# The tail of three attention layers: value blocks, first batch's ending, holding matmuls and a fourth score bank reordered

## The chip, the cores and the metric

The kernel runs on one core of a Trainium2 chip. The metric is the time of one execution on the device in microseconds (us); below that stand times of instructions in one profiled execution, counted from the start of its span. TensorE (PE) does matmuls and transposes into the eight banks of PSUM, VectorE (DVE) and ScalarE (ACT) read these banks, GpSimd (POOL) works in SBUF only, and SyncE (SP) issues most of the DMAs.

## What is computed

The reference is a stack of four blocks on tokens x (2 batches, 512 tokens, 256 wide) with a context of 2 x 1024 rows. Each block adds a gated cross attention and a gated feed-forward part, both on a layer norm of x:

```
x = x + tanh(g_xattn[l]) * attention_l(layernorm(x), context)
x = x + tanh(g_ffn[l])   * ffn_l(layernorm(x))
```

Attention 0 is a windowed one and is not touched. Attentions 1, 2 and 3 are ordinary softmax attentions of 512 queries over 1024 keys, with 16, 16 and 8 heads of 8, 16 and 4 channels, then an output product. The parts behind them are a top-1 mixture of 8 experts (after 1), a gated unit with three hidden layers (after 2) and a token-shift mix (after 3).

## The kernel before

**Tiling.** An attention layer goes through its heads in groups of two (16, 16 and 8 groups; groups of batch 0 first). A group has eight key tiles, called slots here, numbered through the layer: 128, 128 and 64 slots. A slot (group, tile) has two scores, one for each head, 128 keys x 512 queries. The two heads of a group lie on the two row halves of TensorE's array (64 rows each).

**The steps.** `schedule(l)` writes out one list of steps, and every engine walks through the same list and takes its own steps in that order:
- `max`: two matmuls 128 queries x 512 keys into a pair of banks 3 to 6 (L1607), reduced on VectorE (L2394). Their maxima are needed by the scores of later slots, so these products run `LEAD` = 30 scores ahead. When the last is done, the layer has 15 slots left: the tail.
- `score`: one matmul (L1631) into a bank of a ring, and one exponential on ScalarE (L1244) from it into one of six probability buffers. `ring_place()` takes the bank that has been used longest ago. There are three, 0 to 2; in the tail bank 3 joins. A score waits until the exponential that read its bank is done; the first one in bank 3 waits until all reductions of the layer are.
- `values`: a block of 16 matmuls (L1645) for two slots, summed in bank 7 over a group. It waits for the exponentials of its slots, and the first of a group for the copy of the previous group's sums.
- `copy`: ScalarE moves the sums of a group out of bank 7 (L1256), behind the eighth exponential of the next group (slot 3).
- `turned` and `normal`: after every second group the sums are transposed on TensorE (L1661) and copied by ScalarE (L1237), then GpSimd divides by the softmax sums (L976, L977).
- The ending of batch 0: `heads` (transposes of the context, L1678, one for each 128 channels: 1, 2, 1 in layers 1, 2, 3), two `out` (output product, L1705, then VectorE adds to x and takes statistics), `variance` (VectorE, then GpSimd's deviation, L910 and L911), `normalise` (VectorE, L1997) and, in layer 3, two `mix tokens` (transposes, L1686, and on VectorE copies, L2452, and the shift, L2361). These stand in the tail, where banks 4 to 6 are free: `turn()` gives out these three banks in rotation.
- `hold`: a bf16 matmul (L1614) of an identity, whose result nobody reads, in the same rotation.
- In layer 3 `mix` and `mix rest` are a gate product (L1693) that needs the shifted tokens of batch 0.

**The order.** The loop goes by two slots at a time, in the pattern `TILE_PAIR`: maxima, score, maxima, score, score, values, score. The block inside a pair is the one four slots back (`VALUES_LAG`). In the tail there is another one after the pair, when it lags three behind the second slot (`TAIL_LAG`). After the loop the rest of the blocks, the last copy, the last transpose (`context`), its normalisation on VectorE and the ending of batch 1 follow.

In layer 2 VectorE leaves the list after `normalise` of batch 0, enters the branch of the gated unit, casts the first two chunks of its weights (L2640) and takes the rest of the list after that.

Of the kernel before, what the change touches and what calls it, by code (L numbers as in the profile page):

```python
# [15 lines left out]
DC = D // P  # L16
# [23 lines left out]
HG = 2  # L40
KT = M // P
# [10 lines left out]
NGROUPS = {l: B * ATT[l][0] // HG for l in ATT}  # L52
GROUP0 = {l: sum(NGROUPS[i] for i in range(1, l)) for l in range(1, 5)}
EW = {l: ATT[l][0] * ATT[l][1] for l in ATT}
EC = {l: max(1, EW[l] // P) for l in ATT}
PREP0 = {l: sum(EC[i] * CT // CH for i in range(1, l)) for l in range(1, 5)}
QCH0 = {l: sum(EC[i] * T // CH for i in range(1, l)) for l in range(1, 5)}
RING0 = {l: sum(HG * KT * NGROUPS[i] + NGROUPS[i] // 2 - 1 for i in range(1, l)) for l in range(1, 5)}
# [28 lines left out]
CTX_BANKS0 = {0: 0, 1: 2 * DC, 2: 2 * DC + 2 * EC[1], 3: 2 * DC + 2 * EC[1] + 2 * EC[2]}  # L87
HALVES = HG * QT * 2
LEAD = HALVES + 14
VALUES_LAG, TAIL_LAG = 4, 3  # L90
TILE_PAIR = ('maxima', 'score', 'maxima', 'score', 'score', 'values', 'score')
TAIL_HOLDS = 2
WARM_FROM, LEAD_HOLDS = 2, 4
# [9 lines left out]
NORMAL_LAG = 4  # L103
# [12 lines left out]
CTX_SLOT = 7  # L116
# [21 lines left out]
def schedule(l):  # L138

    steps, turns, u, total = [], 0, 0, NGROUPS[l] * HALVES
    batch = NGROUPS[l] // B
    finish = {}
    for b in range(B - 1):
        first = NGROUPS[l] * KT - LEAD // HG + 1
        assert first > (b + 1) * batch * KT + CTX_SLOT
        for i, step in enumerate([("heads", (b, c)) for c in range(EC[l])] + [("out", (b, i)) for i in range(2)]):
            finish[first + i] = step  # L150
        last = first + EC[l] + 2
        finish[last] = ("variance", b)
        finish[last + NORMAL_LAG] = ("normalise", b)
        if l == 3:
            for c in range(DC):
                finish[last + NORMAL_LAG + 2 + c] = ("mix tokens", (b, c))

    def turn(kind, *what):
        nonlocal turns
        steps.append((kind, *what, turns))  # L160
        turns += 1

    def maxima(upto):
        nonlocal u
        while u < min(upto, total):
            steps.append(("max", u))
            u += HG
            steps.extend(LATE[l][v] for v in (u - 1, u) if v in LATE[l])
            if u % HALVES == 0:
                steps.append(("shift", u // HALVES - 1))  # L170
            if WARM_FROM <= u <= LEAD:
                steps.append(("warm",))

    valued, ring, scored = 0, 0, {}
    last_in = {k: None for k in SCORE_BANKS}

    def ring_place():

        nonlocal ring
        if u == total:  # L180
            last_in.setdefault(TAIL_SCORE_BANK, None)
        k = min(last_in, key=lambda k: (-1 if last_in[k] is None else last_in[k], SCORE_BANKS.index(k) if k in SCORE_BANKS else 0))
        before, last_in[k] = last_in[k], ring
        ring += 1
        return k, before

    def values():
        nonlocal valued
        steps.append(("values", valued // KT, valued % KT // 2, scored[valued + 1]))
        valued += 2  # L190

    def score(g, kt, hh):
        steps.append(("score", g, kt, hh, ring_place()))
        if hh < HG - 1:
            return
        sl = g * KT + kt
        scored[sl] = ring
        if kt == COPY_SLOT and g:
            steps.append(("copy", g - 1))
        if kt == CTX_SLOT and g and g % 2 == 0:  # L200
            steps.append(("turned", g - 1, ring_place()))
            steps.append(("normal", g - 1, ring))
        if sl in finish and finish[sl][0] in ("heads", "out", "mix tokens"):
            turn(*finish[sl])
        elif sl in finish:
            steps.append(finish[sl])

    for first in range(0, NGROUPS[l] * KT, 2):
        g, kt = divmod(first, KT)
        places = iter((kt + i, hh) for i in range(2) for hh in range(HG))  # L210
        pairs = iter((first, first + 1))
        for what in TILE_PAIR:
            if what == "maxima":
                maxima(LEAD + HG * next(pairs))
            elif what == "values":
                if valued + VALUES_LAG <= first:
                    values()
            else:
                t, hh = next(places)
                sl = g * KT + t  # L220
                if hh == 0 and u == total and LEAD + HG * (sl - 1) >= total and sl not in finish:
                    for _ in range(TAIL_HOLDS):
                        turn("hold")
                score(g, t, hh)
        if u == total and valued + TAIL_LAG <= first + 1:
            values()
    def first_gate(c):
        turn("mix", c)

    def second_gate(c):  # L230
        steps.append(("mix rest", *next(step[1:] for step in steps if step[:2] == ("mix", c))))

    if l == 3:
        first_gate(0)
    while valued < NGROUPS[l] * KT:
        values()
    if l == 3:
        second_gate(0)
    steps.append(("copy", NGROUPS[l] - 1))
    turn("context", NGROUPS[l] - 1)  # L240
    steps.append(("normal", *steps[-1][1:]))
    if l == 3:
        first_gate(1)
    else:
        steps.append(("tokens", 0))
    for c in range(EC[l]):
        turn("heads", (B - 1, c))
    if l == 3:
        second_gate(1)
    for i in range(2):  # L250
        turn("out", (B - 1, i))
    assert ring == RING0[l + 1] - RING0[l]
    return steps
# [56 lines left out]
def build(nc, io):  # L310
    with ExitStack() as ctx:
# [706 lines left out]
        def _(act):  # L1018
# [185 lines left out]
            def attention(l):  # L1204
# [12 lines left out]
                else:  # L1217
                    act.activation(exp_ready_table[:], onesf[0:1, 0:1], ACT.Exp)

                for step in schedule(l):  # L1220
                    if step[0] == "late tokens":
                        ln_evac(2 * l, [1], -1)
# [149 lines left out]
        def _(pe):  # L1372
# [184 lines left out]
            def attention(l):  # L1557
# [10 lines left out]
                elif l == 1:  # L1568
                    hold_clock(QUERY_HOLDS[l], 1)
                    pe.wait_ge(x_ready, stage * NT)  # L1570
                order = schedule(l)
                rotation = [step for step in order if step[0] in ("context", "heads", "out", "hold", "mix tokens", "mix")]

# [1193 lines left out]
```

## Time and profile before

| | us |
|---|---|
| median of 3 runs | 1056.04 |
| lowest, highest | 1053.68, 1060.72 |
| the profiled execution | 1049.83 |
| its span | 1047.8 |
| busy in the span: TensorE | 958.4 |
| VectorE | 748.3 |
| ScalarE | 510.0 |
| GpSimd | 286.8 |

The mean granted clock of TensorE was 0.969 of full speed (2.4 GHz). A row of instructions in order of time reads: start, time, engine, line, operation, output <- input, shape, count; then in brackets how long the engine stood idle before it, and who released it. "PEld" is the weight load that goes with a matmul. Ends of matmuls are modelled, so starts are the better measure. "Chain of waits" is the chain of work that ended last, followed back from the last instruction.

### The profile page before, as it was taken

How to read it: one execution, taken by the hardware profiler on the slowest of the kernel's cores; microseconds unless marked ns; L12 is line 12 of the kernel's file. 1: busy time of each engine (PE TensorE's matmuls, PEld its weight loads, DVE VectorE, ACT ScalarE, POOL GpSimd, SP SyncE). 2: the span in 40 equal slices, each digit the busy share in tenths (PEclk: the TensorE clock that was granted, in tenths of full speed). 3: DMA queues.
4: the chain of work that ended last, by engine and by line, in shares of the span. 5: the costliest groups of instructions: out<-in, count | busy, mean ns of one | idle time of the engine just before them, and what ended most of it. 6: DMA issues, size and time to landing. Idle time of an engine off the chain costs nothing.

```text
span 1047.8 us, 17509 instructions
## 1 busy us (share of the span) xinstructions
PE 958.4 (91%) x6560; PEld 555.9 (53%) x6560; DVE 748.3 (71%) x1125; ACT 510.0 (49%) x1028; POOL 286.8 (27%) x439
## 2 busy tenths in 40 slices
PE   9897987899999878999689999988999999889898
PEld 4333343444444355999244444444788788544346
DVE  4899888999989332454588899973664645799746
ACT  2672331588888520121027888866312212358763
POOL 3656700233343203002311443421500400023310
PEclk9999989999999977999899999999999999999999
DMA  6789912104320603995341232201254242110001
GB/s 206 248 300 312 357 32 69 43 25 128 120 89 13 182 2 116 319 381 186 101 144 47 71 93 86 52 2 42 89 192 142 83 141 102 29 46 18 2 2 40
DMA packets 79183, 121.83 MB, mean 116 GB/s; under 512 B 9733, under 2 KB 52904, under 8 KB 79090
## 3 DMA queue, kind: packets, MB, share of 16 engines
q1 hardware_dynamic: 59278, 79.29, 24.1%
q10 hardware_dynamic: 19044, 39.22, 10.7%
q0 software_dynamic: 768, 2.10, 0.6%
q8 instruction: 56, 0.92, 0.4%
q14 instruction: 37, 0.30, 0.1%
HBM read 92.10 MB, written 27.81 MB: 114 GB/s over the span
## 4 chain that ended last, share of the span: by engine, by line
PE 64%; DVE 23%; issue 4%; ACT 4%; DMA 2%; POOL 2%; ACTq 1%; DVEq 0%; SPq 0%; POOLq 0%
PE value_bank L1645 12%; PE max_bank L1874 11%; DVE arena L2394 11%; PE st_bank L1631 10%; PE max_bank L1607 7%; PE max_bank L1816 4%; PE st_bank L1804 3%; PE st_bank L1874 2%; ACT arena L1244 2%; PE max_bank L1397 1%; PE st_bank L1553 1%; PE max_bank L1705 1%; DVE arena L2106 1%; PE max_bank L1475 1%; PE st_bank L1661 1%
## 5 line engine op out<-in xcount | busy, mean ns | idle before, releaser
L2394 DVE TENSOR_REDUCE arena<-max_bank 128x2 f32<-128x1024 f32 x320 | 373.3, 1215 | 34.3 <-PE max_bank L1607 31.8
L1244 ACT ACTIVATE arena<-st_bank 128x512 f32<-128x512 f32 x616 | 327.9, 604 | 107.4 <-PE st_bank L1631 99.1
L1645 PE MATMUL value_bank<-arena,vaug 128*9 128x256 f32 (+2 forms) x2560 | 171.2, 386 | 7.8 <-ACT xnT L1256 6.0
L1631 PE MATMUL st_bank<-g_a 64*128 64x512 f32 x456 | 157.7, 447 | 0.0
L1607 PE MATMUL max_bank<-g_a 64*128 64x512 f32 x480 | 133.8, 475 | 14.1 <-DVE arena L2394 12.3
L1874 PE MATMUL max_bank<-g_a,g_w 128*128 128x512 f32 x512 | 117.3, 390 | 1.1 <-POOL g_a L995 1.1
L1631 PEld LDWEIGHTS st_bank<-g_a 64*128 64x128 f32 x456 | 75.4, 185 | 65.0 <-ACT arena L1244 59.5
L1874 PEld LDWEIGHTS max_bank<-g_a,g_w 128*128 128x128 f32 x512 | 95.9, 188 | 21.9 <-POOL g_a L995 2.0
L1645 PEld LDWEIGHTS value_bank<-arena,vaug 128*9 128x9 f32 (+2 forms) x2560 | 56.6, 92 | 85.4 <-issue 27.3
L962 POOL COPY arena<-arena 8x32 f32<-8x32 f32 x160 | 32.1, 200 | 216.6 <-DVE arena L2406 114.2
L1607 PEld LDWEIGHTS max_bank<-g_a 64*128 64x128 f32 x480 | 56.0, 185 | 57.9 <-DVE arena L2394 53.7
L976 POOL TENSOR_TENSOR arena<-arena,minus_one 128x16 f32<-128x16 f32 x17 | 49.3, 2903 | 75.5 <-ACT arena L1237 75.5
L1338 ACT ACTIVATE arena<-max_bank,arena 128x512 f32<-128x512 f32 x32 | 22.0, 688 | 91.7 <-PE max_bank L1874 91.7
L910 POOL TENSOR_SCALAR rstd<-mv 128x4 f32<-128x4 f32 x16 | 3.8, 239 | 202.9 <-DVE mv L1982 202.9
L1631 PE MATMUL st_bank<-g_a,g_x 64*128 64x512 f32 x160 | 58.8, 449 | 0.1
L2617 DVE CAST g_a<-arena 128x512 fp32r<-128x512 f32 x32 | 13.7, 427 | 58.4 <-ACT arena L1338 58.4
L1607 PE MATMUL max_bank<-g_x,g_a 64*128 64x512 f32 x160 | 42.6, 477 | 7.4 <-DVE arena L2394 2.7
L1299 ACT ACTIVATE arena<-st_bank 128x352 f32<-128x352 f32 x24 | 11.1, 464 | 75.6 <-PE st_bank L1804 75.6
L995 POOL TENSOR_TENSOR g_a<-arena,g_a 128x512 fp32r<-128x512 f32 x16 | 23.9, 1493 | 77.6 <-DVE g_a L2678 77.6
L1631 PEld LDWEIGHTS st_bank<-g_a,g_x 64*128 64x128 f32 x160 | 26.7, 189 | 26.1 <-ACT arena L1244 25.9
L1816 PE MATMUL max_bank<-arena 128*128 128x176 f32 x256 | 40.2, 315 | 0.4 <-ACT arena L1299 0.2
L1816 PEld LDWEIGHTS max_bank<-arena 128*128 128x128 f32 x256 | 38.2, 190 | 0.8 <-ACT arena L1299 0.8
(390 smaller groups left out, 1475.0 us busy)
## 6 DMA issues: line engine op xcount, KB each, us to landing
arena<-in_glu_w SPq DMA_DIRECT2D x39, 512.0 KB, 3.2
arena<-kv_table SPq DMA_DIRECT2D x11, 1024.0 KB, 8.1
ctxT<-in_glu_w ACTq DMA_DIRECT2D x22, 512.0 KB, 6.5
arena<-in_w SPq DMA_DIRECT2D x20, 512.0 KB, 6.2
kparts<-arena ACTq DMA_DIRECT2D x12, 512.0 KB, 5.5
arena<-in_w ACTq DMA_DIRECT2D x12, 512.0 KB, 3.4
xnT<-kv_table SPq DMA_DIRECT2D x5, 1024.0 KB, 7.8
g_a<-kparts SPq DMA_DIRECT2D x24, 192.0 KB
```

Of the source, the lines that this page charges most:

```text
L962: ch.link(pool.tensor_copy(mxq[0:HG * QT, r * SQ:(r + 1) * SQ], mxt[gi % 2][r * SQ:r * SQ + HG * QT, :]))
L976: ch.link(pool.tensor_tensor(rsum_p, sums[:, :, :, dh], bc(minus_one[:, 0:1].unsqueeze(2), [P, QT, 2 * HG]), ALU.pow))
L995: pool.tensor_tensor(g_a[0][1][:, f, :], g_tmp[f % 2], g_a[0][0][:, f, :].bitcast(F32), ALU.subtract).then_inc(act_split, 1)
L1244: act.activation(prob[sl % PROBS][:, hh, :], bank[k], ACT.Exp, scale=scale).then_inc(exp_ready, 1)
L1338: ins = act.activation(g_tmp[a % 2], bank[4 + f % 2], ACT.Gelu, scale=gsc[:, 1 + layer, f:f + 1])
L1607: ins = pe.matmul(max_pair[(p + FIRST_PAIR[l]) % len(max_pair)][:, hh, :], Qc[gi % KQ_BUFS][rows, qt * P:(qt + 1) * P], Kc[gi % KQ_BUFS][r ...
L1631: pe.matmul(ring_bank(*place), Kc[gi % KQ_BUFS][rows, kt * P:(kt + 1) * P], Qc[gi % KQ_BUFS][rows, :], start=True, stop=True).then_inc(st_ ...
L1645: ins = pe.matmul(bank[7][at:at + dh + 1, 0:D], vaug[l][:, b * KT + 2 * m + i, h0 + hh, :], tiles[:, a], start=(m == 0 and i == 0), stop=( ...
L1804: ins = pe.matmul(bank[i % 4][:, f % UP_PER_BANK * CAP:(f % UP_PER_BANK + 1) * CAP], mw1[wbuf][:, c, f * P:(f + 1) * P], unit_inT[n % 2][: ...
L1816: ins = pe.matmul(bank[4 + n % 2][:, c * CAP:(c + 1) * CAP], mw2[wbuf][:, f, c * P:(c + 1) * P], hid[n % 2][:, f, :], start=(f == 0), stop ...
L1874: ins = pe.matmul(out, stationary, moving, start=(first and i == 0), stop=(last and i == len(pairs) - 1))
L2394: dve.tensor_reduce(mxh[gi % 2][:, qt:qt + QT + 1:QT, half], max_pair[(p + FIRST_PAIR[l]) % len(max_pair)], AX.X, ALU.max).then_inc(max_re ...
```

## The change

All of it is in `schedule(l)`; no instruction changes but for its place in the list, its bank, and the 48 holds.

- Bank 3 joins the ring only when `tail_ring` places have been given out: not with the second score of the tail's first slot but with the eighth (second score of slot 3 of the last group but one).
- The value block after a pair of slots is gone. Only the one inside the pair stays.
- The two holds before each slot are gone.
- The ending of batch 0 was spread, one step after each slot: heads after slot 2 (and 3 in layer 2), outputs after the next two, variance after the next, normalisation four slots on, mix tokens two and three slots later. Now it stands behind pairs of slots: all heads after slot 3, both outputs after slot 5, variance after slot 7 (behind `turned` and `normal`), normalisation after slot 3 of the last group, both mix tokens after its slot 5.

```diff
-VALUES_LAG, TAIL_LAG = 4, 3
+VALUES_LAG = 4
...
-        first = NGROUPS[l] * KT - LEAD // HG + 1
-        assert first > (b + 1) * batch * KT + CTX_SLOT
-        for i, step in enumerate([("heads", (b, c)) for c in range(EC[l])] + [("out", (b, i)) for i in range(2)]):
-            finish[first + i] = step
-        last = first + EC[l] + 2
-        finish[last] = ("variance", b)
-        finish[last + NORMAL_LAG] = ("normalise", b)
+        first = NGROUPS[l] * KT // 2 - LEAD // HG // 2
+        assert 2 * first > (b + 1) * batch * KT + CTX_SLOT
+        finish[first] = [("heads", (b, c)) for c in range(EC[l])]
+        finish[first + 1] = [("out", (b, i)) for i in range(2)]
+        finish[first + 2] = [("variance", b)]
+        finish[first + 4] = [("normalise", b)]
         if l == 3:
-            for c in range(DC):
-                finish[last + NORMAL_LAG + 2 + c] = ("mix tokens", (b, c))
+            finish[first + 5] = [("mix tokens", (b, c)) for c in range(DC)]
...
+    tail_ring = RING0[l + 1] - RING0[l] - HG * (LEAD // HG - 2)
...
-        if u == total:
+        if u == total and ring >= tail_ring:
             last_in.setdefault(TAIL_SCORE_BANK, None)
...
-        if sl in finish and finish[sl][0] in ("heads", "out", "mix tokens"):
-            turn(*finish[sl])
-        elif sl in finish:
-            steps.append(finish[sl])
...
                 t, hh = next(places)
-                sl = g * KT + t
-                if hh == 0 and u == total and LEAD + HG * (sl - 1) >= total and sl not in finish:
-                    for _ in range(TAIL_HOLDS):
-                        turn("hold")
                 score(g, t, hh)
-        if u == total and valued + TAIL_LAG <= first + 1:
-            values()
+        for step in finish.get(first // 2, []):
+            turn(*step) if step[0] in ("heads", "out", "mix tokens") else steps.append(step)
```

The tail of layer 1 before and after, pair by pair (s: a score, V: a value block, numbered in the tail, h: two holds). Layer 2 has a second heads step; in layer 3 (groups 6 and 7) the mix tokens and the gate product come in addition.

```
slots      before                                            after
14.0-1     s s(bank 3) s V1 s V2                             s s s V1 s
14.2-3     s s heads s s copy out V3                         s s s V2 s(bank 3) copy heads
14.4-5     s s out s s variance V4                           s s s V3 s out out
14.6-7     h s s h s s turned normal V5                      s s s V4 s turned normal variance
15.0-1     h s s s s normalise V6                            s s s V5 s
15.2-3     h s s h s s copy V7                               s s s V6 s copy normalise
15.4-5     h s s h s s V8                                    s s s V7 s
15.6-7     h s s h s s V9                                    s s s V8 s
after      V10                                               V9 V10
```

## Rows read from the trace of the kernel before

**Rows 1.** Page: busy time of the engines, and the chain's shares by engine.
```profile
PE 958.4 (91%) x6560; PEld 555.9 (53%) x6560; DVE 748.3 (71%) x1125; ACT 510.0 (49%) x1028; POOL 286.8 (27%) x439
PE 64%; DVE 23%; issue 4%; ACT 4%; DMA 2%; POOL 2%; ACTq 1%; DVEq 0%; SPq 0%; POOLq 0%
```

**Rows 2.** Chain of waits, layer 1, before the tail: start, time, work (us).
```profile
337.43 0.98 PE value_bank L1645 x16
340.03 0.98 PE value_bank L1645 x16
```

**Rows 3.** Instructions in order of time, start of each tail: start, time; idle before.
```profile
341.71 2.36 DVE L2394 TENSOR_REDUCE arena<-max_bank 128x2 f32<-128x1024 f32 x2 [0.24 <-PE max_bank L1607]
344.12 0.49 PE L1631 MATMUL max_bank<-g_a 64*128 64x512 f32 x1 [2.10 <-DVE arena L2394]
694.87 2.36 DVE L2394 TENSOR_REDUCE arena<-max_bank 128x2 f32<-128x1024 f32 x2 [0.24 <-PE max_bank L1607]
697.28 0.50 PE L1631 MATMUL max_bank<-g_a 64*128 64x512 f32 x1 [2.10 <-DVE arena L2394]
988.49 2.36 DVE L2394 TENSOR_REDUCE arena<-max_bank 128x2 f32<-128x1024 f32 x2 [0.23 <-PE max_bank L1607]
990.90 0.50 PE L1631 MATMUL max_bank<-g_a 64*128 64x512 f32 x1 [2.08 <-DVE arena L2394]
```

**Rows 4.** Stretches, busy time by engine and clock (layers 1, 3); one block.
```profile
344.00:348.00 4.00, 3.88 (x31) 1.39 (x35) 0.45 (x3) 1.68 (x3) 1.53 (x6) 0.59 0.02 5
992.00:996.00 4.00, 3.65 (x35) 1.63 (x28) 1.20 (x2) 2.80 (x7) 1.01 (x4) 1.00 0.01 2
344.54 1.76 PE L1645 MATMUL value_bank<-arena,vaug 128*9 128x256 f32 x16
```

**Rows 5.** Order of time, layers 3 and 2: the small costs of a tail.
```profile
992.31 0.50 PE L1631 MATMUL st_bank<-g_a 64*128 64x512 f32 x1
992.74 1.05 PE L1645 MATMUL value_bank<-arena,vaug 128*5 128x256 f32 x16
998.21 1.13 PE L1705 MATMUL max_bank<-wo,xnT 32*128 32x256 f32 x4
1002.13 0.63 PE L1661 MATMUL st_bank<-ident,xnT 128*128 128x128 f32 x4 [0.16 <-ACT arena L1244]
1004.88 1.57 ACT L1244 ACTIVATE arena<-st_bank 128x512 f32<-128x512 f32 x3
704.67 1.99 PE L1705 MATMUL max_bank<-wo,xnT 128*128 128x256 f32 x8
```

**Rows 6.** Order of time, layer 1: copy, first value block of the last group.
```profile
363.05 0.47 ACT L1256 ACTIVATE xnT<-value_bank 128x256 f32<-128x256 f32 x1
363.66 1.05 PE L1645 MATMUL value_bank<-arena,vaug 128*9 128x256 f32 x16 [1.83 <-ACT xnT L1256]
```

**Rows 7.** All instructions of line L1614: shortest, median, longest in ns.
```profile
L1614 PE MATMUL max_bank<-identb x48: 376/387/388, 355.5 to 1013.1; 64*128 64x512 bf16 x48
```

**Rows 8.** Order of time: last value block of layers 1, 2 and 3.
```profile
369.69 1.05 PE L1645 MATMUL value_bank<-arena,vaug 128*9 128x256 f32 x16 [0.72 <-ACT arena L1244]
724.15 1.06 PE L1645 MATMUL value_bank<-arena,vaug 128*17 128x256 f32 x16 [0.73 <-ACT arena L1244]
1015.62 1.05 PE L1645 MATMUL value_bank<-arena,vaug 128*5 128x256 f32 x16
```

**Rows 9.** Order of time: GpSimd and VectorE in the tails of layers 3, 2.
```profile
1003.73 2.90 POOL L976 TENSOR_TENSOR arena<-arena,minus_one 128x16 f32<-128x16 f32 x1 [0.70 <-ACT arena L1237]
1003.14 1.38 DVE L1997 TENSOR_SCALAR xn<-x,mv,rstd 128x256 f32<-128x256 f32 x4 [1.54 <-POOL rstd L911]
1011.01 0.69 DVE L2452 COPY xnT<-max_bank 128x512 f32<-128x512 f32 x1 [2.62 <-PE max_bank L1686]
1013.44 0.75 DVE L2361 SCALAR_TENSOR_TENSOR arena<-xnT,arena 128x511 f32<-128x511 f32 x1
717.10 1.30 DVE L2640 CAST g_w<-arena 128x1024 fp32r<-128x1024 f32 x2 [2.89 <-issue]
```

## Prediction

> **What bounds the kernel now.** I read the page first: TensorE is busy for 91% of the span, and the chain that ended last runs 64% of the time through it, 23% through VectorE [rows 1]. That is a mean over stages, so I looked for the stretches that the change touches: the last fifteen slots of each attention layer, after the last row-maximum product. The chain of waits just ahead of such a stretch shows the normal rhythm: one value block of 0.98 us in every two tiles, 2.60 us from block to block (337.43 to 340.03), TensorE never idle for long [rows 2]. The rest, 1.62 us, holds eight half-height matmuls (four maxima, four scores), so a pair on the two row halves takes 0.40 to 0.43 us.
>
> Then the tail. I measure it from the start of the last two reductions on VectorE to the end of the layer's last value block. The reductions start at 341.71, 694.87 and 988.49 [rows 3], the last value blocks end at 370.74, 725.21 and 1016.67 [rows 8], so the tails take 29.03, 30.34 and 28.18 us. Their scores (29 at half of 0.43), ten value blocks, transposes and two output products make about 20 us of TensorE work in layer 1, and 29 exponentials at 0.52 us or less (three in 1.57 us [rows 5]) with three copies make 16.5 us on ScalarE. So no engine is full; the tail is bound by its order. Two places show it. At its start, the first score into bank 3 waits for all reductions: 2.10, 2.10 and 2.08 us of idle TensorE [rows 3]. And the first value block of a group waits for the copy of the previous group's sums, which stands on ScalarE behind four exponentials whose scores were just issued: 1.83 us in layer 1 [rows 6].
>
> **The change, part by part.** *Bank 3 used later.* The first seven tail scores go round banks 0 to 2. Their exponentials are nearly up to date, so the 2.1 us wait on VectorE is gone; bank 3 is first used by the last score of slot 3, some 4 us later, when the reductions (2.36 us [rows 3]) are over. What is late next is the three-bank ring itself: a score waits for the exponential three back.
>
> *Value blocks only inside two tiles.* Each block is now four slots behind its scores and stands before the fourth score; the block after the fourth score is gone, so two blocks instead of one remain after the last pair of tiles. In exchange three scores of the next group stand ahead of the block that waits for the copy.
>
> *Holds.* 48 matmuls go [rows 7]. Each lasts 0.39 us, two of them overlap on the two row halves, and most ran where TensorE waited anyway, so I take no separate term: the walk below simply has none.
>
> *First batch's ending.* Heads after slot 3, both outputs after slot 5 in a row, variance after slot 7, normalisation four slots later. The work is the same. ScalarE starves for about 1.5 us during the two outputs, where TensorE is busy anyway. On GpSimd the deviation now stands behind the context normalisation (2.90 us [rows 9]).
>
> I now walk layer 1's new order, in us after the start of the last two reductions, with durations from these rows: value block 0.98, a pair of scores on opposite halves 0.43, a lone one also 0.43 (992.31 to 992.74), a group of four transposes 0.57 to 0.63, a pair of tiles' output product 1.06 (row duration 1.13), a score's exponential just behind its 0.50, the block behind a copy 0.61 us after the copy's start (363.05 to 363.66) [rows 5, 6]. The ten value blocks start at:
> - block 1: 0.85, after two scores.
> - block 2: 3.45. Gap 2.6: with three banks the score before it waits for an exponential that could not start before block 1 ended.
> - block 3: 6.25. Gap 2.8: block, lone score, heads 0.57, then a score pair and a lone score. The copy of the sums is over by then.
> - block 4: 10.65. Gap 4.4: block, score, two outputs (2.12), scores.
> - block 5: 13.55. Gap 2.9: block, score, turn 0.63, scores.
> - block 6: 15.4. Gap 1.85: 0.98 and two pairs of scores, four banks.
> - block 7: 18.15. Gap 2.75: its copy stands behind the fourth exponential and ends at 18.0. About 0.7 us of TensorE idleness remains.
> - blocks 8, 9, 10: 20.0, 21.4, 22.4, then the end at 23.4.
>
> ScalarE's last exponential ends near 22.2, so the doubled rest of value blocks costs little: it is TensorE work with nothing missing. Layer 1: 29.0 - 23.4 = 5.6 us gained. Of this, 1.6 us is the half clock that the old tail suffered: after the idle stretch the granted clock was 0.59 over four microseconds, and a value block took 1.76 us [rows 4], while in layer 3 the same gap left it at 1.00. Two blocks ran in that stretch, each 0.71 longer than 1.05, and a score between them: 1.6 us, an estimate.
>
> Layer 2 has two head chunks (0.57 more) and outputs of 1.99 instead of 1.13 us (1.72 more for two) [rows 5]: 25.7 against 30.34, a gain of 4.6 us. VectorE is tight there: normalisation ends near 22.4 (turn at 15, its copy to about 15.5, GpSimd's 2.90 and the product behind it, together some 3.7, then 1.54 for the deviation and 1.38 for the normalisation), the branch idles it 2.89 us, two casts take 1.30 [rows 9], so it is free at 26.6, just before the last turn at 26.9. If it is late, it costs up to 1 us.
>
> Layer 3: up to block 7 as layer 1. Both token transposes then stand together after slot 5 (from 19.6 to 20.75; the normalised tokens are there at 19.5). VectorE copies them one after the other; from the second copy's start to the end of the second shift took 3.18 us (1011.01 to 1014.19 [rows 9]), so the first gate product can start at 24.3. TensorE reaches it at 23.0. Here is a new wait of 1.3 us with the last two value blocks queued behind it. End at 24.35 + 1.06 + 2.05 = 27.5, against 28.18: 0.7 us gained.
>
> Sum: 5.6 + 4.6 + 0.7 = 10.9 us. What follows each tail is a chain of transposes, outputs and statistics in the same order, so nothing that I see takes the gain back. The profiled execution took 1049.83 us and would take 1038.9; it lies 0.6% below the median of 1056.04, from which the same sum gives 1045.1. I take **1045 us**. Bounds of the unsure terms: the three-bank stretch 1 us to either side per layer, the clock 0 to 1.6 us in each of three layers, layer 3's wait 0 to 3 us.
>
> **The rule on the clock.** In rows: clock 1.00 up to 344, then 0.59 after 2.1 us without a matmul [rows 3, 4]. The Trainium skill, "TensorE: Matmul & The Clock Gate", section "What's actually happening", says that the throttled state is the default and that activity releases it; the drop in layer 1 agrees, the unchanged clock in layer 3 does not. By it this change, which takes out matmuls that do nothing but keep TensorE active, could bring the half clock back. In the walk TensorE has no gap above 1.3 us, less than the 2.1 us that went ahead of the one drop, so I leave it out of the sum and make it the rival with the opposite sign.
>
> **The rivals.**
> - *Slower: half clock in the tails.* Place: from the outputs of the first batch on, where TensorE has gaps and no holds. Price: 13 us of its work per layer would take 26, three layers 39, less 10.9: 28 slower, 1084 us. It decides as soon as more than 10.9 us of work, 3.6 per layer, runs at 1.2 GHz; over 1% slower from 21 us on. Against it: the first half of the old tails had no holds either (the first of the 48 stands at 355.5, 13.8 us into layer 1's tail [rows 7]), and only one of three dropped.
> - *Half the gain.* Only the opening waits (2.1 us, three times, 6.3) come back, and the ring of three banks, the two outputs in a row and layer 3's gate take 1 to 2 of it: 4 to 5 less, 1051 to 1052. For it: TensorE and ScalarE need nearly the same time for two tiles (1.84 against four exponentials in 2.0), so every hand-over counts.
> - *More than forecast.* Ordinary runs lie 6 us above the profiled one; if the half clock after the opening wait strikes in layers 2 and 3 there (1.6 each), and the hand-over of a group also loses all its 1.8 us: 14 to 19 less, about 1040.
> - *No change in effect:* the tails end as before because something else ends them. Nothing shows it; it is in the second rival.
>
> **Chances.** A per cent, 10.6 us, is about what can be told from no change. Forecast (8 to 14 less) 0.50, of which 0.27 lie past one per cent; more 0.17; half or nothing 0.24; slower by the clock 0.09. So faster 0.44, same 0.47, slower 0.09. The range leaves out the clock case and the outer edge of the others: 1037 (19 less) to 1055 (1 less).
>
> **What would show it.** After the change, no score waits 2 us for L2394; the tails measure about 23.4, 25.7 and 27.5 us; the granted clock stays 1.00 at 344 to 348; at the first block of a group TensorE waits under 1 us for L1256; in layer 3 the first gate (L1693 in the old numbering) waits about 1.3 us for L2361. Wrong if the clock falls in a tail, if value blocks wait for exponentials each time, or if the gate waits over 3 us.

## The result

The changed kernel takes 1041.63 us (1040.82 to 1043.56, 4 runs) against 1056.04 (1053.68 to 1060.72, 4 runs, one more than in the table above): a ratio of 0.9861, 95% interval 0.9824 to 0.9898. 1045 was forecast, with a range of 1037 to 1055: the direction and the range hold, the gain is 14.4 us where 10.9 were summed. Beside a later set of runs of the kernel before (1058.74, 17 runs) the same kernel gave 1045.36 us and 0.9881 (0.9844 to 0.9919). One of these 17 runs was in a slower state of the chip; medians and lowest to highest times here and below count such runs, ratios leave them out.

The profiled execution took 1042.29 us, only 7.5 less than its counterpart. The tails say more. Measured as in the prediction, they took 22.42, 24.65 and 26.30 us, together 73.37 instead of 87.55. In a second profile of the same kernel they were 22.43, 24.66 and 26.32.

Page of the changed kernel, the span and part 1:

```profile
span 1040.6 us, 17413 instructions
PE 959.9 (92%) x6512; PEld 557.3 (54%) x6512; DVE 748.1 (72%) x1125; ACT 510.4 (49%) x1028; POOL 287.0 (28%) x439
```

The busy time of the whole span says little here, because it also grows where the clock is lower. Within the three tails TensorE was busy for 72.11 us before and 69.27 after, and idle for 15.44 before and 4.10 after: of the 14.2 us that the tails save, 11.3 are idle time. Of the other 2.8, 1.7 are the half clock in layer 1 (an estimate: 29.03 us at a mean granted clock of 0.94). Instructions of the changed kernel in order of time, start of the three tails (against [rows 3]; L2385 was L2394, L1622 was L1631):

```profile
345.32 2.36 DVE L2385 TENSOR_REDUCE arena<-max_bank 128x2 f32<-128x1024 f32 x2 [0.23 <-PE max_bank L1598]
348.32 0.49 PE L1622 MATMUL st_bank<-g_a 64*128 64x512 f32 x1 [0.45 <-ACT arena L1235]
694.78 2.36 DVE L2385 TENSOR_REDUCE arena<-max_bank 128x2 f32<-128x1024 f32 x2 [0.23 <-PE max_bank L1598]
697.79 0.50 PE L1622 MATMUL st_bank<-g_a 64*128 64x512 f32 x1 [0.45 <-ACT arena L1235]
984.33 2.36 DVE L2385 TENSOR_REDUCE arena<-max_bank 128x2 f32<-128x1024 f32 x2 [0.23 <-PE max_bank L1598]
987.33 0.49 PE L1622 MATMUL st_bank<-g_a 64*128 64x512 f32 x1 [0.45 <-ACT arena L1235]
```

The wait of 2.1 us for VectorE is gone in all three; the ring of three banks costs one wait of 0.45 us for an exponential. The granted clock (third number from the right) of layer 1's first eight microseconds, against 0.59 in [rows 4]:

```profile
344.00:348.00 4.00, 3.87 (x39) 1.52 (x31) 3.70 (x5) 2.96 (x7) 0.00 (x0) 1.00 0.01 4
348.00:352.00 4.00, 3.68 (x37) 1.76 (x41) 0.82 (x2) 3.27 (x8) 1.53 (x6) 1.00 0.01 2
```

The copy and the first value block of layer 1's last group, against [rows 6], and the first batch's outputs with the exponential behind them:

```profile
362.04 0.38 ACT L1247 ACTIVATE xnT<-value_bank 128x256 f32<-128x256 f32 x1
362.57 1.05 PE L1636 MATMUL value_bank<-arena,vaug 128*9 128x256 f32 x16 [0.39 <-ACT xnT L1247]
```

```profile
352.81 1.99 PE L1696 MATMUL max_bank<-wo,xnT 128*128 128x256 f32 x8
355.32 1.58 ACT L1235 ACTIVATE arena<-st_bank 128x512 f32<-128x512 f32 x3 [1.81 <-PE st_bank L1622]
```

The block waits 0.39 us where it waited 1.83. ScalarE idles for 1.81 us during the outputs, as foreseen, and TensorE does not. The last value blocks of layers 1, 2 and 3 (two at a time, L1636), against [rows 8]:

```profile
365.77 1.97 PE L1636 MATMUL value_bank<-arena,vaug 128*9 128x256 f32 x32
717.47 1.96 PE L1636 MATMUL value_bank<-arena,vaug 128*17 128x256 f32 x32
1008.72 1.91 PE L1636 MATMUL value_bank<-arena,vaug 128*5 128x256 f32 x32
```

Layer 3, VectorE and TensorE before the first gate product, against [rows 9]:

```profile
1001.47 1.38 DVE L1988 TENSOR_SCALAR xn<-x,mv,rstd 128x256 f32<-128x256 f32 x4 [5.17 <-POOL rstd L902]
1006.85 0.75 DVE L2352 SCALAR_TENSOR_TENSOR arena<-xnT,arena 128x511 f32<-128x511 f32 x1
1007.66 1.12 PE L1684 MATMUL max_bank<-arena 128*128 128x512 f32 x2 [1.57 <-DVE arena L2352]
```

That is the forecast wait, 1.57 us instead of 1.3. In layer 2 VectorE just makes it, as forecast: its casts end at 720.26, the last turn wants it at 720.63.

**Where the other 7 us of the profile went.** The tails save 14.2 us, the span 7.2. Layer 1's tail starts 3.6 us later (345.32 against 341.71), from its end to layer 2's tail there are 2.9 us more, from there to layer 3's 1.6 more, and behind layer 3's tail 1.2 less. All these stretches hold the same instructions. Most of the first 3.6 us arise between 124 and 141 us (VectorE's instructions are 0.6 us late at the one and 3.6 at the other), where the clock fell in the changed kernel and not in the kernel before. No changed step has run by then, so this is not the change's doing. The same four microseconds before, then after (the granted clock is third from the right):

```profile
136.00:140.00 4.00, 4.00 (x24) 3.53 (x22) 3.29 (x10) 2.09 (x3) 0.00 (x0) 1.00 0.01 4
```

```profile
136.00:140.00 4.00, 4.00 (x13) 2.75 (x12) 2.78 (x9) 3.06 (x5) 0.00 (x0) 0.50 0.03 6
```

The 1.6 us more and the 1.2 us less go with the clock too (0.99 after the change against 1.00 before, and 1.00 against 0.95). The 2.9 us do not: the clock was 0.94 in both. Their place is the hand-over of the experts' results: the last store is issued at 499.18 before and at 495.95 after, 3.2 us earlier, but the gather on GpSimd starts at 503.09 and 502.51. Before, then after:

```profile
499.18 0.34 SPq L837 DMA_DIRECT2D slot_out<-arena  x1
503.09 1.00 POOL L1014 DMA_INDIRECT xn<-slot_out,arena  x1 [10.99 <-SPq L845]
```

```profile
495.95 0.34 SPq L828 DMA_DIRECT2D slot_out<-arena  x1
502.51 1.00 POOL L1005 DMA_INDIRECT xn<-slot_out,arena  x1 [13.64 <-SPq L836]
```

3.9 us passed the one time and 6.6 the other, with the DMA engines busy in both. In the fourteen profiles of this study this wait took anything in between, and layer 1's tail began anywhere from 341.7 to 349.0 us, whatever was changed in the tails; the mean granted clock up to there was 0.97 at the earliest start (before) and 0.94 at the latest (k_after_spread). So the clock outside the tails and this wait are noise of several microseconds on one execution, and below I compare tails from profiles and whole times from medians.

### The profile page after: what moved, and what is told of

It reads as the page before. It is cut to its first block, busy times and chain, and to the rows that moved or that the text cites. A ratio compares the mean times of both kernels' runs of the same rounds, so it can differ in the third digit from the quotient of the medians.

```text
span 1040.6 us, 17413 instructions
## 1 busy us (share of the span) xinstructions
PE 959.9 (92%) x6512; PEld 557.3 (54%) x6512; DVE 748.1 (72%) x1125; ACT 510.4 (49%) x1028; POOL 287.0 (28%) x439
## 3 DMA queue, kind: packets, MB, share of 16 engines
HBM read 92.10 MB, written 27.81 MB: 115 GB/s over the span
## 4 chain that ended last, share of the span: by engine, by line
PE 63%; DVE 22%; issue 5%; DMA 4%; ACT 3%; POOL 2%; ACTq 1%; DVEq 0%; SPq 0%; POOLq 0%
PE value_bank L1636 12%; PE max_bank L1865 11%; PE st_bank L1622 11%; DVE arena L2385 10%; PE max_bank L1598 7%; PE max_bank L1807 4%; PE st_bank L1795 3%; DMA kparts<-arena 3%; PE st_bank L1865 2%; PE max_bank L1388 1%; PE max_bank L1696 1%; PE st_bank L1544 1%; DVE arena L2097 1%; PE st_bank L1652 1%; PE max_bank L1795 1%
## 5 line engine op out<-in xcount | busy, mean ns | idle before, releaser
L2385 DVE TENSOR_REDUCE arena<-max_bank 128x2 f32<-128x1024 f32 x320 | 373.5, 1216 | 36.0 <-PE max_bank L1598 33.9
L1636 PE MATMUL value_bank<-arena,vaug 128*9 128x256 f32 (+2 forms) x2560 | 170.6, 385 | 1.2 <-ACT xnT L1247 1.2
L1622 PE MATMUL st_bank<-g_a 64*128 64x512 f32 x459 | 151.7, 441 | 1.4 <-ACT arena L1235 1.4
L1598 PE MATMUL max_bank<-g_a 64*128 64x512 f32 x480 | 134.3, 475 | 14.4 <-DVE arena L2385 12.6
L1622 PEld LDWEIGHTS st_bank<-g_a 64*128 64x128 f32 x459 | 72.9, 184 | 68.9 <-ACT arena L1235 65.0
L1636 PEld LDWEIGHTS value_bank<-arena,vaug 128*9 128x9 f32 (+2 forms) x2560 | 56.4, 92 | 78.7 <-issue 28.2
L1622 PE MATMUL st_bank<-g_a,g_x 64*128 64x512 f32 x160 | 59.2, 453 | 0.1
L1622 PEld LDWEIGHTS st_bank<-g_a,g_x 64*128 64x128 f32 x160 | 27.1, 192 | 26.8 <-ACT arena L1235 26.4
L1988 DVE TENSOR_SCALAR xn<-x,mv,rstd 128x256 f32<-128x256 f32 x64 | 23.0, 423 | 25.4 <-POOL rstd L902 25.2
```

The lines of the kernel that those rows point to most:

```text
L1598: ins = pe.matmul(max_pair[(p + FIRST_PAIR[l]) % len(max_pair)][:, hh, :], Qc[gi % KQ_BUFS][rows, qt * P:(qt + 1) * P], Kc[gi % KQ_BUFS][r ...
L1622: pe.matmul(ring_bank(*place), Kc[gi % KQ_BUFS][rows, kt * P:(kt + 1) * P], Qc[gi % KQ_BUFS][rows, :], start=True, stop=True).then_inc(st_ ...
L1636: ins = pe.matmul(bank[7][at:at + dh + 1, 0:D], vaug[l][:, b * KT + 2 * m + i, h0 + hh, :], tiles[:, a], start=(m == 0 and i == 0), stop=( ...
L1988: dve.tensor_scalar(xn[:, t, :], x[:, t, :], mv[:, t, 0:1], rstd[:, t:t + 1], ALU.subtract, ALU.mult).then_inc(xn_ready, 1)
L2385: dve.tensor_reduce(mxh[gi % 2][:, qt:qt + QT + 1:QT, half], max_pair[(p + FIRST_PAIR[l]) % len(max_pair)], AX.X, ALU.max).then_inc(max_re ...
```

## Experiments

All tails in us, measured as above. "Sum" is of one profile each. The clock fell in some tails and not in others, so the next column takes that out: from each tail it takes off the tail's length times what its mean granted clock lacks to 1.00. This is an estimate. It supposes that TensorE was busy while the clock was halved, and it was for over nine tenths of that time.

| kernel | layer 1 | 2 | 3 | sum | at full clock | ratio to before (95%) |
|---|---|---|---|---|---|---|
| before | 29.03 | 30.34 | 28.18 | 87.55 | 85.84 | |
| after | 22.42 | 24.65 | 26.30 | 73.37 | 73.37 | 0.9861 (0.9824 to 0.9898) |
| a_bank | 25.47 | 29.87 | 26.17 | 81.51 | 79.80 | 0.9944 (0.9906 to 0.9982) |
| b_values | 25.14 | 28.13 | 28.46 | 81.73 | 80.02 | 0.9963 (0.9916 to 1.0011) |
| c_holds | 26.84 | 33.95 | 29.11 | 89.90 | 83.07 | 1.0007 (0.9962 to 1.0053) |
| d_ending | 30.81 | 34.93 | 35.11 | 100.85 | 90.61 | 1.0080 (1.0038 to 1.0122) |
| e_after_bank | 25.03 | 25.72 | 31.77 | 82.52 | 75.94 | 0.9900 (0.9861 to 0.9938) |
| f_after_values | 29.77 | 29.49 | 31.39 | 90.65 | 80.41 | 0.9980 (0.9941 to 1.0019) |
| g_after_holds | 24.45 | 25.70 | 27.81 | 77.96 | 77.96 | 0.9862 (0.9789 to 0.9936) |
| k_after_spread | 22.07 | 25.09 | 23.53 | 70.69 | 70.69 | 0.9809 (0.9736 to 0.9882) |
| after_again | 22.43 | 24.66 | 26.32 | 73.41 | 73.41 | 0.9881 (0.9844 to 0.9919) |
| m_earlier_mix | 22.43 | 24.65 | 24.11 | 71.19 | 71.19 | 0.9835 (0.9801 to 0.9870) |
| q_pairs | 22.42 | 25.07 | 22.72 | 70.21 | 70.21 | 0.9818 (0.9785 to 0.9851) |
| r_keep | 28.89 | 30.33 | 28.17 | 87.39 | 85.68 | 0.9978 (0.9949 to 1.0007) |

### One part of the change alone

**a_bank:**

```diff
-        if u == total:
+        if u == total and ring >= tail_ring:
             last_in.setdefault(TAIL_SCORE_BANK, None)
```

> The kernel before with one part of the change: bank 3 joins the score ring seven places later. The three tails took 29.03, 30.34 and 28.18 us before (87.6 in all) and 22.42, 24.65 and 26.30 us after the whole change (73.4). Theory 'order' (the gain is the sum of several small waits): the three opening waits of 2.1 us go, and the half clock of layer 1 with them (1.6 us), while the second value block, which still follows the first pair, waits about 1 us for exponentials in the three-bank ring: tails 5 us shorter in all, about 82.5. Rival 'opening' (the change is this part and nothing else): tails about 74, time as after the change, 14 us below before. Rival 'nothing': the wait moves to the value block, tails within 1 us of 87.6.

The sum fell by 6.0 us, where "order" said 5; "opening" and "nothing" fall. The half clock of layer 1 went, but in layer 2 it came late in the tail (1.7 us), so the 6.0 us are the same at full clock.

**b_values:**

```diff
-        if u == total and valued + TAIL_LAG <= first + 1:
-            values()
```

> The kernel before with one part of the change: no value block after a pair of slots, only the one inside it. Theory 'order': the first block of a group no longer stands right behind the scores whose exponentials precede its copy, so the 1.0 to 1.9 us waits for the copy at each group's start shrink to about 0.5, twice per tail; the opening wait of 2.1 us stays, two more blocks stand at the end. Tails 5 us shorter in all, about 82.5. Rival 'opening': no effect or 1 us longer, since two blocks instead of one follow the last exponential. If both a_bank and this give 5 and 5, the parts add up with the holds.

5.8 us less, and as much at full clock: "order" again. Layer 3 gained nothing because its opening wait was followed by half clock in this profile, which cost 1.7 us.

**c_holds:** the three lines that put two holds ahead of a slot are deleted.

> The kernel before without its 48 holding matmuls, nothing else changed. Theory 'order': they ran mostly where TensorE waited, so tails 0 to 2 us shorter in all and no more half clock than before. Rival 'clock': without them the granted clock falls to about 0.6 in the second half of the tails, each tail 3 us or more longer.

The sum rose by 2.35 us, and the ratio of the times is 1.0007. But layer 1, at full clock, is 2.2 us shorter than before, about 0.5 of it beyond the half clock of the kernel before, and at full clock the three tails are 2.8 us shorter: the holds did cost time, as "order" said. Its second half, no more half clock than before, failed. The clock fell behind the opening waits of layers 2 and 3, and once more near the end of layer 2's tail (699.02 to 732.98) behind a wait for a copy. In c_holds, layer 2, two stretches at the start, then the block behind that wait:

```profile
699.00:703.00 4.00, 1.91 (x14) 0.64 (x18) 2.74 (x4) 1.61 (x4) 0.86 (x5) 0.80 0.00 0
703.00:707.00 4.00, 4.00 (x31) 1.23 (x23) 0.00 (x0) 0.94 (x2) 0.67 (x2) 0.50 0.01 4
```

```profile
725.02 1.69 PE L1642 MATMUL value_bank<-arena,vaug 128*17 128x256 f32 x16 [1.83 <-ACT xnT L1253]
```

The first two are at a tail's start, where neither kernel had holds. The third is in the second half, as "clock" wanted, but in one layer of three, and the same happened with the holds in place (a_bank and d_ending in layer 2, r_keep in layer 1). The whole runs lean towards "clock": the mean granted clock was 0.9550 in the ten of c_holds and 0.9595 in the 24 of the kernel before that its ratio is taken from, up to 5 us more lost (an estimate, 0.0045 of 1060), which can outweigh the 2.8 us that the tails gain. So in the old order the holds may have kept the clock up somewhat; this run does not settle it.

**d_ending:** the ending stands behind pairs of slots as in the change; the block after the pair, the early bank 3 and the holds stay.

```diff
-        if sl in finish and finish[sl][0] in ("heads", "out", "mix tokens"):
-            turn(*finish[sl])
...
+        for step in pairs_done.get(first // 2, []):
+            turn(*step) if step[0] in ("heads", "out", "mix tokens") else steps.append(step)
```

> The kernel before with one part of the change: the first batch's ending in two places (heads behind slot 3, both outputs behind slot 5, variance behind slot 7, normalisation four slots on, in layer 3 both token transposes together behind slot 5 of the last group). The holds stay at the slots where they were. Theory 'order': layers 1 and 2 within 0.5 us of before, layer 3 longer by 1 to 2 us, because the gate product waits for VectorE's shift. Rival: the two outputs in a row, which leave ScalarE idle, cost 1.5 us in each layer, tails 4 to 5 us longer.

A miss of both theories: 13.3 us longer, and slower by the median (1.0080). 8.5 of it are half clock, which came once in layer 1 and twice in layers 2 and 3. At full clock 4.8 us are left, +1.8, -0.5 and +3.5 by layer: the rival's total, but not its 1.5 us in each layer. Layer 1 of d_ending shows the waits:

```profile
354.20 1.64 PE L1653 MATMUL value_bank<-arena,vaug 128*9 128x256 f32 x16 [2.35 <-ACT xnT L1264]
362.11 0.39 PE L1622 MATMUL max_bank<-identb 64*128 64x512 bf16 x1 [0.50 <-DVE x L2449]
```

In the kernel before, the heads and the first output stood between the scores and the block that waits for the copy, and filled its wait. Moved behind the pair they come after that block: it waits 2.35 us with the heads queued behind it. A hold also waits 0.50 us, because its bank comes round from an output that VectorE has not yet added. Grouping the ending is a loss while the trailing block stays.

### One part of the change undone

**e_after_bank** (`if u == total:` again), **f_after_values** (the trailing block again), **g_after_holds** (two holds where they were), **k_after_spread** (the old places of the ending). The second is

```diff
+        if u == total and valued + 3 <= first + 1:
+            values()
         for step in finish.get(first // 2, []):
```

> The changed kernel with one part undone: bank 3 joins the ring at the start of the tail again. Theory 'order': the second score of the tail waits for the last reduction again, 2.1 us in each layer; tails 6.3 us longer than the 73.4 of the change, about 79.7, and in one or the other layer the half clock comes back (1.6 us more). Rival: ScalarE and TensorE catch up on the way, tails 2 us longer or less.

9.15 us longer, of which 6.6 are half clock: once in layer 1, behind the opening, and twice in layer 3. There the first dip came nine microseconds after the opening wait, while TensorE was busy, the second behind the gate product's wait of 1.57 us. The first line is the opening wait, the second the first dip's first value block, the third the last two value blocks in the second dip, which took 1.91 us in the changed kernel:

```profile
992.13 0.50 PE L1622 MATMUL max_bank<-g_a 64*128 64x512 f32 x1 [2.09 <-DVE arena L2385]
1001.04 1.49 PE L1636 MATMUL value_bank<-arena,vaug 128*5 128x256 f32 x16
1018.20 3.29 PE L1636 MATMUL value_bank<-arena,vaug 128*5 128x256 f32 x32
```

Layer 2, without a dip, lost only 1.1 us of the 2.1, and at full clock all three together lose 2.6. So the rival had the order right (2 us or less), TensorE catches up, and what "order" said of the half clock came in a larger size.

> The changed kernel with one part undone: the value block after a pair of slots is back. Theory 'order': the waits for the copy at each group's first block return (1.0 to 1.9 us, two per tail), and in the three-bank stretch the second block waits about 1 us; one block fewer stands at the end. Tails 4 to 6 us longer, about 78. Rival 'opening': within 1 us of 73.4.

17.3 us longer, three times what was expected, and 10.2 of it are half clock; at full clock 7.0 are left, a little over the forecast. Layer 1 of f_after_values:

```profile
352.05 1.67 PE L1638 MATMUL value_bank<-arena,vaug 128*9 128x256 f32 x16 [2.35 <-ACT xnT L1249]
366.65 1.90 PE L1638 MATMUL value_bank<-arena,vaug 128*9 128x256 f32 x16 [1.83 <-ACT xnT L1249]
```

Both first blocks of a group wait for their copy, and behind both the block itself takes 1.67 and 1.90 us instead of 1.05: half clock. With this part undone the median is that of the kernel before (0.9980). By the sum at full clock it is the largest part of the gain.

> The changed kernel with the 48 holds back at the slots where they were (two before a slot's first score). Theory 'order': TensorE waits little now, so each pair of holds costs about 0.2 to 0.4 us on its path: 24 pairs, tails 3 to 6 us longer than 73.4. Rival 'clock': they keep the clock up, tails shorter. Rival 'hidden': within 1 us, as in the kernel before.

4.6 us longer: "order". The wait of d_ending for VectorE is here too (0.49 us in layer 1). The clock was 1.00 in all tails with and without the holds, so "clock" falls for this order. The medians cannot tell 4.6 us apart with four runs.

> The changed kernel with the first batch's ending spread out again, one step behind each slot (heads behind slot 2, outputs behind the next two, variance, normalisation four slots on, token transposes two and three slots later). Theory 'order': layer 3's wait of 1.57 us before the gate product goes, layers 1 and 2 stay within 0.5 us: tails 1.5 us shorter in all, about 72. Rival: grouping itself saves something, because single scores between other matmuls cost 0.43 us like pairs: tails longer by 0.2 us per step, 2 to 3 us in all.

2.7 us shorter. Layer 3 gives 2.8 (26.30 to 23.53), and the gate wait is gone there; layer 1 gains 0.35 and layer 2 loses 0.4. The grouping is the one part that costs something: "order" is right in kind, the size was too small.

### The gate, the pairs, the clock

> The changed kernel once more, beside the three below. The tails should again measure about 22.4, 24.7 and 26.3 us with the granted clock at 1.00 throughout. Theory 'gaps' (the old order opened gaps of 1.8 to 2.4 us on TensorE, after which the clock often fell, at random; the new order has none above 1.6): its executions lie close together, within 0.5% from lowest to highest, while those of the kernel before spread over 1% or more. Rival: both spread alike.

The tails repeat within 0.02 us. The spread does not obey: 1039.78 to 1049.58, 0.9%, against 1.4% of the 16 runs of the kernel before that its ratio is taken from (1051.77 to 1066.65). That half of "gaps" is missed. The spread goes with the clock of the whole run: the fastest of these six runs had a mean granted clock of 0.967, the slowest 0.958, which is worth up to 9.4 us (an estimate, 0.009 of 1045) of the 9.8 between them, and the tails had none of it.

**m_earlier_mix:**

```diff
-        finish[first + 1] = [("out", (b, i)) for i in range(2)]
-        finish[first + 2] = [("variance", b)]
-        finish[first + 4] = [("normalise", b)]
+        finish[first + 1] = [("out", (b, i)) for i in range(2)] + [("variance", b)]
+        finish[first + 3] = [("normalise", b)]
...
-            finish[first + 5] = [("mix tokens", (b, c)) for c in range(DC)]
+            finish[first + 4] = [("mix tokens", (b, c)) for c in range(DC)]
```

> The changed kernel with three steps earlier: variance right behind the outputs, so that GpSimd does it before the context normalisation, normalisation of batch 0 two slots earlier, in layer 3 both token transposes behind slot 3 of the last group instead of slot 5. Theory 'gate' (layer 3's gate product waits 1.57 us for VectorE's shift): the wait goes and layer 3's tail is 1.5 to 2 us shorter, about 24.5; the token transposes fill part of the wait for the copy. Layers 1 and 2 unchanged within 0.2. Rival: the last value blocks then wait for exponentials, layer 3 gains under 0.5.

Layer 3: 2.2 us shorter, layers 1 and 2 unchanged. VectorE's last shift starts before the gate's place in the order, and the product follows without a wait; m_earlier_mix, VectorE then TensorE:

```profile
1006.04 0.75 DVE L2351 SCALAR_TENSOR_TENSOR arena<-xnT,arena 128x511 f32<-128x511 f32 x1
```

```profile
1007.19 1.12 PE L1683 MATMUL max_bank<-arena 128*128 128x512 f32 x2
```

**q_pairs** (on k_after_spread):

```diff
-        for what in TILE_PAIR:
+        for what in (('score', 'score', 'values', 'score', 'score') if u == total else TILE_PAIR):
```

> The spread ending of the previous study (tails 22.07, 25.09, 23.53) with another order inside two tiles of the tail: score, score, value block, score, score, instead of three scores, block, score. Theory 'pairs' (a lone score between other matmuls takes 0.43 us like a pair on both row halves, so the old order takes 1.08 us for four scores and this one 0.86): 0.2 us less where TensorE sets the pace, about 1 us less per tail, about 68 in all. Rival 'exponentials' (four exponentials set the pace at 2.0 us for two tiles): no gain, and the last value block waits 0.5 us more, tails about 71 to 72.

Layer 3 gained 0.8 us, layer 1 lost 0.35, layer 2 stayed: between the two theories, nearer "exponentials". It has the lowest median of all, 1038.93 us, 0.9818 of before; next to the change's 0.9881 in the same runs the intervals just touch, and its base k_after_spread (0.9809, four runs) cannot be told apart from it.

**r_keep** (on the kernel before):

```diff
+            if TAIL_SCORE_BANK not in last_in:
+                steps.append(("keep", *min((before, k) for k, before in last_in.items())))
...
+                        pe.wait_ge(exp_ready, RING0[l] + step[1] + 1)
+                        hold_clock(KEEP, step[2])
```

> The kernel before with nine bf16 matmuls of 512 columns (about 1.9 us of TensorE work whose result nobody reads) put into each tail's opening wait of 2.1 us, in a free score bank. The wait itself stays. Theory 'gaps' (the clock falls at random after this gap, in about half of the openings seen so far): no opening is followed by half clock, the three tails are about 85.5 to 86.5 instead of 87.6, the median is 2 us or more below before and the runs spread less. Rival: the clock falls for another reason, and dips stay as frequent.

The opening of layer 1 with the gap filled, and its clock:

```profile
345.43 2.12 PE L1379 MATMUL st_bank<-identb 128*128 128x512 bf16 x9
347.60 0.50 PE L1634 MATMUL max_bank<-g_a 64*128 64x512 f32 x1
```

```profile
345.20:349.20 4.00, 3.94 (x30) 1.51 (x28) 2.73 (x4) 1.90 (x4) 0.89 (x5) 1.00 0.01 4
```

No opening of the three dipped. If each had its 7 in 15 chance (counted below), that would still happen by luck one time in seven. The sum missed its forecast because the clock fell elsewhere, in layer 1 behind the 1.84 us wait for the last copy:

```profile
365.59 1.90 PE L1648 MATMUL value_bank<-arena,vaug 128*9 128x256 f32 x16 [1.84 <-ACT xnT L1259]
```

The median is 2 us below before, its interval reaches 1.0007: not settled by time.

## Why the prediction was right, and where its sizes were off

- **Bank 3 used later.** Right. The three waits of 2.1 us became 0.45; alone the part is worth 6.0 us, undoing it costs 9.15, or 2.6 at full clock.
- **Value blocks inside the pair.** Right in mechanism: the waits for copies shrank from 1.83 to 0.39 us (layer 1) and two blocks at the end cost nothing.
- **The parts and the whole.** As measured, the parts alone give -6.0, -5.8, +2.35 and +13.3 us, which is nowhere near -14.2. Most of that is the clock. At full clock they are -6.0, -5.8, -2.8 and +4.8, together -9.9, and undone one by one +2.6, +7.0, +4.6 and -2.7, together 11.5, against 12.5 for the whole change (85.84 to 73.37). So 1 to 3 us in all are coupling between parts. A single part shifts more: bank 3 is worth 6.0 us alone and 2.6 when all else is changed. What the walk did not see is that an order with waits of 2 us in it also pays in half clock: up to 10.2 us in d_ending and in f_after_values.
- **Holds.** The walk had none, rightly. That they cost 4.6 us in the new order, with a wait for a bank of their own rotation, was not seen.
- **The walk.** Its gaps between block starts in layer 1 were 2.6, 2.8, 4.4, 2.9, 1.85, 2.75, 1.85, 1.4. Measured: 2.6, 2.65, 4.0, 2.65, 2.0, 2.5, 1.8, 1.4. The mis-sized term is the cost around other steps: the outputs were put at 1.06 each where the eight products take 1.92 together before the next score, and three scores in a row at 0.86 where they take 0.66. The end comes 1.0 us early in layer 1, 1.05 in layer 2 and 1.2 in layer 3: 3.2 us of the 3.5 that the forecast fell short. That the rest is so small is in part luck: outside the tails the two profiles differ by 7 us for other reasons, and the later runs put the gain at 13.4 us between medians (1058.74 to 1045.36).
- **The gate of layer 3.** Right in place; 1.57 us for 1.3. m_earlier_mix removed it.
- **The half clock, as a rival of the opposite sign.** It did not come: no tail of any kernel with the change's opening and without the trailing block had a dip, in after, after_again, g, k, m and q (18 tails). Counted over all profiles, the opening wait of 2.1 us (before, b, c, d, e: 15 tails) was followed by half clock in its first eight microseconds 7 times; with the wait filled (r_keep) or gone (a_bank) 0 of 6. Of the 20 waits of 1.8 to 2.4 us for a copy (before, a, c, d, f, r) 10 had half clock in them or right behind them; of the 8 of 1.0 to 1.25 us (before, a, c, r) none. The gate's wait of 1.57 us, which the change brought in, had it in e_after_bank and not in after or after_again. Single edits point to the waits as the cause: e and f each put waits back into the changed kernel, and the dips came with them. Why one wait is followed by a dip and the next is not stays open, and one dip of e_after_bank stands behind busy microseconds. In the new order the missing holds cost no clock (1.00 with them and without); in the old one they may have (c_holds). The Trainium skill ("TensorE: Matmul & The Clock Gate", "What's actually happening") has the throttled state as the default that activity releases; the counts above agree with it, while the slower result that it would have given here for taking out the holds did not come.
- **Chances.** The half-gain rival did not happen; the "more than forecast" case, 14 to 19 less, is where the median lies, if at its edge; its reason, half clock behind the openings of layers 2 and 3 in ordinary runs, was seen in profiles of other kernels with that opening and not in the one of before. The interval, 1.0 to 1.8% less, lies past the one per cent that the prediction set as its line.

## What to carry to other kernels

When an order is written out by hand, walk the whole new order on the critical engine with durations from rows, and look for every wait of about 2 us that an edit leaves or makes: in e_after_bank and f_after_values such waits cost more through the clock (6.6 and 10.2 us) than by the order itself (2.6 and 7.0). Before adding up parts, take the half clock out of each profile. Ahead of a block that waits for a copy, put scores or outputs that TensorE can run meanwhile. And a filler matmul that takes its turn in a bank rotation inherits the waits of that rotation.

## What was not expected of the hardware

- Waits of TensorE of about 2 us were followed by half clock (1.2 GHz) about every second time: 7 of 15 openings of 2.1 us, 10 of 20 waits of 1.8 to 2.4 us for a copy, none of 8 waits of 1.0 to 1.25 us. One such dip cost 1.7 us or more (an estimate, before: 29.03 us at 0.94); the two of layer 2 in c_holds, granted clock 0.85 over the tail, 5.1.
- The time of a whole run follows its mean granted clock. In the first set of runs of the kernel before, 1050.54 us went with 0.971 and 1065.91 with 0.953.
- The wait for the experts' last store varied between 3.9 and 6.6 us for the same transfer, and the start of layer 1's tail by 7 us between profiles. Medians of four runs tell less about a 3 us edit than one pair of traces: tails without half clock repeat to 0.02 us.
